# A transformer layer with mixture of experts: the expert tiles moved behind most of the attention, and the norms and ScalarE's work put in another order

## The reference

```python
x = x + layernorm(attention1(layernorm(x), keys, values))     # x: (8, 512, 128); 16 heads of 8, relu projections
x = x + layernorm(encoder(layernorm(x)))

def encoder(x):                       # L = 8 is the sequence, N = 512 tokens are the batch
    y1 = ln(x + mha(x), ln1_g, ln1_b)       # 4 heads of 32, softmax over the 8 rows of the batch axis
    y2 = ln(y1 + moe(y1), ln2_g, ln2_b)
def moe(x):                           # x as 4096 tokens of 128 features, 8 experts
    gates = softmax(x @ wg); idx = argmax(gates); mask = one_hot(idx)
    loc = position of the token among those of its expert; keep = loc < 512
    y = (x @ w1[e] + b1[e]) @ w2[e] + b2[e]     # no activation between: one matrix per expert
    out = gate_val * y if keep else 0
```

## Time and profile before

| | |
|---|---|
| median of 3 runs | 705.54 us (703.77 to 711.51) |
| profiled execution | 711.12 us, span 709.3 us |
| busy over the span | TensorE 562.8 us, VectorE 525.9, ScalarE 396.8, GpSimd 217.1 |
| granted clock of TensorE, mean | 0.88 (1.00 is 2.4 GHz, 0.50 is 1.2 GHz) |

### The profile page before, as it was taken

How to read it: one execution, slowest core, us unless ns; L and a number is a source line. 1 busy time by engine, 2 the same in 40 slices (tenths; PEclk the granted TensorE clock), 3 DMA queues, 4 the chain that set the end, 5 groups by cost and what they waited for, 6 DMA issues and landing times.

```text
span 709.3 us, 9793 instructions
## 1 busy us (share of the span) xinstructions
PE 562.8 (79%) x3475; PEld 206.4 (29%) x3475; DVE 525.9 (74%) x882; ACT 396.8 (56%) x775; POOL 217.1 (31%) x312
## 2 busy tenths in 40 slices
PE   2874999999999999999999777746787588996600
PEld 2650222222222222222222246542444134331100
DVE  4869799999999999999996147495144522869966
ACT  1560699988988889888887523522221110023352
POOL 6001010293324503542228229232220400005341
PEclk9995699999999999999999989966798775978655
DMA  9732011112210112102200020000000000000022
GB/s 251 225 122 101 18 33 34 37 32 63 62 38 28 49 50 62 33 23 70 66 19 10 8 70 1 2 0 0 1 1 0 1 0 1 0 0 0 2 59 59
DMA packets 31393, 28.94 MB, mean 41 GB/s; under 512 B 6240, under 2 KB 23784, under 8 KB 31344
## 3 DMA queue, kind: packets, MB, share of 16 engines
q1 hardware_dynamic: 29312, 27.33, 13.1%
q10 hardware_dynamic: 2032, 0.98, 0.5%
HBM read 19.23 MB, written 8.65 MB: 39 GB/s over the span
## 4 chain that ended last, share of the span: by engine, by line
PE 52%; DVE 25%; ACT 9%; POOL 6%; issue 4%; DMA 2%; ACTq 0%; SPq 0%; DVEq 0%
PE ps L1459 12%; PE ps L1454 9%; PE ps L590 9%; DVE row_max L1631 9%; PE ps L1427 5%; DVE space L922 3%; PE ps L588 3%; PE ps L545 2%; ACT space L835 2%; ACT attended L1579 2%; PE ps L614 2%; ACT space L1563 1%; DVE space L268 1%; DMA w_in<-in_L_ffn_out_proj_w 1%; POOL space L391 1%
## 5 line engine op out<-in xcount | busy, mean ns | idle before, releaser
L1631 DVE TENSOR_REDUCE row_max<-ps 128x2 f32<-128x1024 f32 x256 | 299.4, 1218 | 16.4 <-PE ps L1427 13.6
L1563 ACT ACTIVATE space<-ps 128x512 f32<-128x512 f32 x512 | 271.8, 605 | 47.8 <-PE ps L1454 47.3
L1454 PE MATMUL ps<-space 51*128 51x512 bf16 x512 | 159.0, 387 | 6.6 <-ACT space L1563 3.3
L1459 PE MATMUL ps<-space 128*32 128x512 f32 x1024 | 138.1, 612 | 3.0 <-ACT space L1563 0.7
L1427 PE MATMUL ps<-space 48*128 48x512 bf16 x512 | 128.1, 400 | 14.2 <-DVE row_max L1631 12.5
L590 PE MATMUL ps<-W,space 128*128 128x512 f32 x128 | 89.5, 788 | 0.0
L1454 PEld LDWEIGHTS ps<-space 51*128 51x128 bf16 x512 | 41.1, 94 | 164.6 <-ACT space L1563 144.8
L922 DVE TENSOR_REDUCE space<-ps 128x128 f32<-128x1024 f32 x32 | 39.0, 1220 | 62.4 <-PE ps L590 62.4
L1303 POOL CAST max_parts<-row_max 128x16 bf16<-128x16 f32 x32 | 6.3, 198 | 239.9 <-DVE row_max L1631 239.8
L437 POOL TENSOR_TENSOR space<-PC,same_row 128x512 f32<-128x512 f32 x32 | 32.9, 1059 | 80.1 <-DVE PC L881 80.1
L588 PE MATMUL ps<-c_stack,space 32*128 32x512 bf16 x64 | 28.0, 437 | 24.2 <-DVE space L922 22.7
(11 more groups left out here) (223 smaller groups left out, 708.2 us busy)
## 6 DMA issues: line engine op xcount, KB each, us to landing
q_parts_dram<-space SPq DMA_DIRECT2D x2, 1536.0 KB, 5.4
space<-q_parts_dram SPq DMA_DIRECT2D x64, 48.0 KB
attended_dram<-attended SPq DMA_DIRECT2D x128, 18.0 KB
X<-in_L_attn_queries SPq DMA_DIRECT2D x8, 256.0 KB, 7.6
space<-in_L_ffn_w SPq DMA_DIRECT2D x2, 1024.0 KB, 5.9
space<-q_parts_dram SPq DMA_DIRECT2D x64, 32.0 KB
space<-attended_dram SPq DMA_DIRECT2D x16, 128.0 KB, 2.4
space<-inverses_dram SPq DMA_DIRECT2D x16, 128.0 KB
```

The lines of the kernel that those rows point to most:

```text
L1454: pe.matmul(ps[:, col_bank(v), :], k_rows[rows_a, kappa // 4 % 2, tc * P:(tc + 1) * P], q_stack[rows_a, kappa % 4, b * S:(b + 1) * S], sta ...
L1459: mm = pe.matmul(ps[32 * m:32 * m + 32, PV, :], v_heads[:, tc, PAIR * (kappa // 4) + m % PAIR, :], probs[:, tc % 2, m, :], start=(tc == 0) ...
L1563: act.activation(probs[:, tc % 2, m, :], ps[:, col_bank(v), :], ACT.Exp, scale=1.0 / math.sqrt(DH)).then_inc(s_pr, 1)
L1631: dve.tensor_reduce(row_max[:, par].rearrange("p (a c) -> p a c", a=PAIR)[:, :, item], ring(n), AX.X, MAX).then_inc(s_free, 1)
```

## The change

Tile 0 comes first in half 6. Tiles 0, 1 and 2 stand in half 6 and 3 and 4 in half 7; tiles 0 to 7 take turns in banks 0/1 and 2/3, which the scores no longer need once the last of them are reduced, and all later ones in three pairs of banks. The second part of `spread_turned` uses banks 6 and 7 in every half. The norms of the groups are split into a beginning (`variance1`) and an end (`apply1`), with other work between; the two norms of the last group are begun before the first residual and finished behind it. The second group's tokens are turned ahead of the second scores. The gate weights are begun after selection 21 (23 before). GpSimd's additions on 128 x 1024 are done as two halves. In the tail, variances and scales are in a new order and the last group's fifth norm has buffers of its own. ScalarE's order follows.

In the diff, lines that are only removed in the orders of TensorE, ScalarE and VectorE are left out; they stand in the kernel above.

```diff
...
 BIG = 1e30
-RING = [0, 2, 4]
-EARLY = 2 * B
+EARLY = B
 MASK_ROW = PARTS
...
+def st65(g):
+    return st6 if g == G - 1 else st6p
+def small5(g):
+    return small if g == G - 1 else smallp
...
-LAST1, LAST2, NORM4 = G + 1, G + 2, 2 * G + 2
-LN1 = [G] + [G + 2 + g for g in range(1, G)]
-TAIL = [(4, 0), (4, 1), (5, 0), (4, 2), (5, 1), (5, 2), (4, 3), (5, 3)]
+LAST1, LAST2, NORM4 = G, G + 2, 2 * G + 2
+LN1 = [G + 1] + [G + 2 + g for g in range(1, G)]
+TAIL = [(4, 0), (4, 1), (5, 0), (4, 2), (5, 1), (4, 3), (5, 2), (5, 3)]
...
+    def affine(g, gain, shift, done):
+        for row, op in ((gain, MUL), (shift, ADD)):
+            for lo in (0, QB):
+                half = A[:, g, lo:lo + QB]
+                ins = pool.tensor_tensor(half, half, bcast(rows[:, row, :], QB), op)
+                if op == MUL or lo == 0:
+                    ch.done(ins)
+                else:
+                    ins.then_inc(done, 1)
+            ch.wait()
...
         pool.wait_ge(s_n3, g + 1)
-        ch.done(pool.tensor_tensor(A[:, g], A[:, g], bcast(rows[:, 0, :], B), MUL))
-        ch.wait()
-        pool.tensor_tensor(A[:, g], A[:, g], bcast(rows[:, 1, :], B), ADD).then_inc(s_y1, 1)
+        affine(g, 0, 1, s_y1)
...
         pool.wait_ge(s_wa, g)
-        pool.tensor_tensor(same(A[:, g]), same(A[:, g]), same(YT[:, g]), ADD).then_inc(s_sum, 1)
+        for lo in (0, QB):
+            half = A[:, g, lo:lo + QB]
+            ins = pool.tensor_tensor(half, half, YT[:, g, lo:lo + QB], ADD)
+            ins.then_inc(s_sum, 1)
...
         pool.wait_ge(s_n4, g + 1)
-        ch.done(pool.tensor_tensor(A[:, g], A[:, g], bcast(rows[:, 2, :], B), MUL))
-        ch.wait()
-        pool.tensor_tensor(A[:, g], A[:, g], bcast(rows[:, 3, :], B), ADD).then_inc(s_aff, 1)
+        affine(g, 2, 3, s_aff)
...
-    return 6 if k < EARLY else RING[(k - EARLY) % len(RING)]
+    return 2 * (k % 2) if k < EARLY else 2 * ((k - EARLY) % 3)
...
-    bank, lo = ((6, 0), (5, B * E), (5, B * E), (7, 0))[g]
+    bank, lo = (5, B * E) if g < 2 else (7, 0)
     return ps[:, bank, lo:lo + P // 2].bitcast(BF16)
-LOGITS_BANK = [5, 5, 5, 6]
+LOGITS_BANK = [5, 5, 6, 6]
...
         pe.wait_ge(s_y1, g + 1)
         turn(A[:, g], 6, s_y1t)
+    def tile(k):
+        if k < 2:
+            pe.wait_ge(s_msk, 2 * G)
+        elif k < EARLY:
+            pe.wait_ge(s_sel, k - 1)
+        elif k == EARLY + 2:
+            pe.wait_ge(s_ot, 2 * G)
+            pe.wait_ge(s_lgc, 2)
+        else:
+            pe.wait_ge(s_sel, k - 1 if k < EARLY + 2 else k - 2)
+        if k % B == 0:
+            pe.wait_ge(s_nm, k // B + 1)
+        experts(k)
     first_group(pe, 7)
     pe.wait_ge(s_rm, 1)
     pe.wait_ge(s_qkv, 3)
     scores2(0)
     pe.wait_ge(s_rows, 16 * 6)
     pe.wait_ge(s_pr, COLUMN_ITEMS)
     turn_tokens(1)
+    scores2(1)
+    pe.wait_ge(s_pve, NQ)
     project(1)
+    pe.wait_ge(s_cb, QB)
+    for q in range(2 * G):
+        g, half = q // QPG, q % QPG
         if q >= 1:
             pe.wait_ge(s_ot, q)
+        if q in (0, 2, 4):
+            pe.wait_ge(s_qkv, 3 * (g + 1) + 2)
+        if q in (5, 7):
+            pe.wait_ge(s_lgc, q // 2 - 1)
+        if q == 6:
+            pe.wait_ge(s_nm, 1)
         spread_turned(q, 0, 4)
+        if half == 0:
+            if g < G - 1:
+                pe.wait_ge(s_qkv, 3 * (g + 1) + 3)
+            if g:
+                pe.wait_ge(s_res, g)
         spread_turned(q, 1, 6)
+        if q + 2 < 2 * G:
+            scores2(q + 2)
+        if q == 6:
+            tile(0)
+            tile(1)
+        if q == 7:
+            tile(3)
         attend(q)
         if q == 1:
             project_out(0)
             turn_tokens(2)
             project(2)
         if q == 3:
             turn_y1(0)
+            pe.wait_ge(s_y1c, 2)
             project_out(1)
             turn_tokens(3)
             project(3)
+        if q == 4:
+            route(0)
+        if q == 5:
+            turn_mask(0)
+            turn_y1(1)
+            pe.wait_ge(s_y1c, 4)
+            project_out(2)
+        if q == 6:
+            route(1)
+            tile(2)
+        if q == 7:
+            turn_mask(1)
+            tile(4)
+            project_out(3)
+    for k in range(5, EARLY):
+        tile(k)
+    pe.wait_ge(s_res, G)
+    turn_y1(2)
+    tile(8)
+    tile(9)
+    route(2)
+    tile(10)
+    tile(11)
+    turn_mask(2)
+    for k in range(12, 16):
+        tile(k)
+    for half in range(2):
+        if half == 0:
+            pe.wait_ge(s_lgc, 3)
+        else:
+            pe.wait_ge(s_nm, 3)
+        pe.wait_ge(s_y1l, half + 1)
+        for b in range(QB):
+            mm = pe.transpose(ps[:, 6 + half, b * P:(b + 1) * P], A[:, G - 1, QB * half + b, :], ident[:])
+        mm.then_inc(s_y1t, 1)
+        tile(16 + half)
+    route(G - 1)
+    tile(18)
+    tile(19)
     turn_mask(G - 1)
     pe.wait_ge(s_lgc, G)
     masks = maskp[:].rearrange("p g k c -> p (g k) c")[:, :, MASK_ROW:MASK_ROW + 2 * E]
     pe.matmul(ps[:, 6, 0:T * E], upper[:], masks, start=True, stop=True)
     pe.matmul(ps[:, 6, T * E:2 * T * E], all_ones[:], masks, start=True, stop=True).then_inc(s_cnt, 1)
+    for k in range(20, T):
+        tile(k)
 def back_end_act(act):
     def copy_tokens(g, bank=4):
...
     copy_tokens(1)
     softmax_exp(0)
+    project(1, lambda: softmax_exp(1))
+    copy_turned(0, 0, 4)
+    copy_turned(0, 1, 6)
+    copy_attended(0)
+    softmax_exp(2)
+    copy_turned(1, 0, 4)
+    copy_turned(1, 1, 6)
+    copy_attended(1)
+    softmax_exp(3)
     copy_tokens(2)
+    root(act, LAST1, smallo)
+    project(2, lambda: root(act, LN1[0]))
     copy_turned(2, 0, 4)
     copy_turned(2, 1, 6)
     copy_attended(2)
+    root(act, LAST2, smallo)
     copy_turned(3, 0, 4)
     copy_turned(3, 1, 6)
     softmax_exp(4)
     copy_attended(3)
     copy_y1(0, 6)
+    softmax_exp(5)
+    copy_tokens(3)
+    project(3, lambda: root(act, LN1[1]))
+    copy_turned(4, 0, 4)
+    copy_turned(4, 1, 6)
+    copy_attended(4)
+    softmax_exp(6)
     copy_logits(0)
     copy_turned(5, 0, 4)
+    copy_turned(5, 1, 6)
+    copy_attended(5)
+    softmax_exp(7)
     copy_y1(1, 6)
+    copy_turned(6, 0, 4)
+    copy_turned(6, 1, 6)
+    root(act, LN1[2])
+    copy_attended(6)
     copy_logits(1)
     copy_turned(7, 0, 4)
+    copy_turned(7, 1, 6)
+    copy_attended(7)
+    root(act, LN1[3])
     copy_y1(2, 6)
     copy_logits(2)
     for half in range(2):
         act.wait_ge(s_y1t, G + half)
         act.copy(same(YT[:, G - 1, QB * half:QB * half + QB]), ps[:, 6 + half, :]).then_inc(s_y1c, 1)
...
     apply4 = lambda g, which=range(B): apply(g, s_i4, small4(g), s_n4, which)
-    apply5 = lambda g, which=range(B): apply(g, s_i5, smallp, s_n5, which)
+    apply5 = lambda g, which=range(B): apply(g, s_i5, small5(g), s_n5, which)
     root4 = lambda g: root(act, tail(4, g), small4(g))
-    root5 = lambda g: root(act, tail(5, g), smallp)
+    root5 = lambda g: root(act, tail(5, g), small5(g))
...
     apply5(1)
+    root4(3)
+    apply4(3, range(0, B, 2))
     root5(2)
     apply5(2)
-    root4(3)
-    apply4(3, range(0, B, 2))
     root5(3)
...
-    def ln1(g):
+    def variance1(g):
         dve.wait_ge(s_res, g + 1)
-        norm(dve, ch, LN1[g], tiles(A, g), tiles(A, g)).then_inc(s_n3, 1)
+        norm_variance(dve, ch, tiles(A, g), st6, small)
+    def apply1(g):
+        norm_invert(dve, ch, LN1[g], small)
+        norm_apply(dve, tiles(A, g), tiles(A, g), small).then_inc(s_n3, 1)
...
         dve.tensor_reduce(YT[:, k // B, k % B, :], ps[:, bank:bank + 2, :].rearrange("p a (d e) -> p (a d) e", e=E),
                           AX.X, MAX).then_inc(s_sel, 1)
+    last = G - 1
     compact(0)
     normalise(0)
+    dve_invert(dve, last)
     for q in range(1, 2 * QPG):
         compact(q)
         normalise(q)
+    dve.wait_ge(s_r1, G)
+    norm_variance(dve, ch, tiles(A, last), st6o, smallo)
     residual(0)
+    variance1(0)
+    norm_invert(dve, ch, LAST1, smallo)
+    ch.done(norm_apply(dve, tiles(A, last), tiles(A, last), smallo))
+    ch.wait()
+    ch.done(dve.tensor_tensor(X[:, last], X[:, last], A[:, last], ADD))
+    apply1(0)
+    ch.wait()
+    norm_variance(dve, ch, tiles(X, last), st6o, smallo)
     compact(4)
+    norm_invert(dve, ch, LAST2, smallo)
+    norm_apply(dve, tiles(X, last), tiles(A, last), smallo).then_inc(s_n2l, 1)
     normalise(4)
     compact(5)
     normalise(5)
+    residual(1)
+    variance1(1)
+    apply1(1)
     compact(6)
     normalise(6)
+    choose(0)
     compact(7)
     normalise(7)
+    copy_others(0)
+    residual(2)
+    variance1(2)
+    select(0)
+    apply1(2)
+    select(1)
+    select(2)
+    choose(1)
+    select(3)
+    select(4)
+    copy_others(1)
     g = G - 1
     residual(g)
     dve.wait_ge(s_res, G)
     norm_variance(dve, ch, tiles(A, g), st6, small)
+    select(5)
     norm_invert(dve, ch, LN1[g], small)
     for lo in (0, QB):
         bs = range(lo, lo + QB)
...
```

(117 more changed lines are left out.)

70 lines of the change are left out of this document (2 added, 68 removed).

## The result

The changed kernel takes 663.61 us (median of 4 runs, 657.12 to 663.98) against 707.16 for the kernel before on the same occasions. The ratio is 0.936, interval 0.928 to 0.944: faster. The forecast was 660. The profiled execution took 663.98 us, 47.1 less than the one before, where I had forecast 46.

The account below looks back on a forecast made before the run. TensorE and VectorE waited on each other over one bank pair between residuals 1 and 3; stages gave -62, slow clock +16, so -46: 665 us profiled, 660 as median, range 639 to 684.

Parts of the forecast that it names:

- 26.4 + 26.1 + 58.1: Residual 1 to 2, 2 to 3 and 3 to gate: forecast us at full clock, against 68.8, 58.7 and 26.4 before.
- the clock's +16: TensorE ahead of the gate: 28% of 22 tiles slow costs 14 us, one slow projection 2 more.
- The idle 2.5 us for the last group's choice: Residual 3 to gate: TensorE stands 2.5 us until the last group's choice is made.
- Sum -8.7, to 65.9: Gate to end: two more selections +2.4, halved additions -7.5, earlier variances and own buffers -3.6.
- Halves of 1.17 us leave about half of it: Tail: halving GpSimd's additions cuts about 15 us of VectorE's stall excess by 7.5, bounds 0 and -9.
- waits of 3.3 and 2.4 us shrink: Tail: variances begun ahead of tiles and separate scale buffers for the last group shorten waits, -3.6 us.
- rival (c): Tail gives nothing back: VectorE gets in only behind both halves, selections eat the variances' gain; 669 us, chance 0.07.
- (a): Clock worse than now: attention halves without tiles idle TensorE, 60% of 22 tiles slow; 680 us, chance 0.13.
- (d): Slower than before: 22 tiles ahead of the gate in a row, all at 1.2 GHz; 716 us, chance 0.03.
- I take 0: Start of back end to residual 0: earlier attention half used up by VectorE's statistics; 0 us, bounds -3.4 and +2.
- -10.2 for the norms: Residual 0 to 1: last group's norms fill VectorE's 8.9 us root wait; bounds -6 and -12 us.
- Rival (b): Engine orders don't interlock: ScalarE stands at roots, two waits of 8.9 us give +18; 678 us, chance 0.14.

Follow-up runs that it names:

- b: Changed kernel with the tail's order of variances, scales and roots and the fifth norm's shared buffers as before, halved additions kept: 659.72 us, ratio 0.935.
- d: Changed kernel with the norms at the start of the back end in one piece again, ScalarE's roots moved to match: 664.43 us, ratio 0.939.
- i: Changed kernel with only the start of the back end as before (second scores ahead of the turned tokens, second exponential behind the projections): 662.72 us, ratio 0.937.
- j: Changed kernel with front, norms, GpSimd's additions and tail order undone together, leaving the tile move: 672.25 us, ratio 0.951.
- f: Changed kernel with all 32 expert tiles in one pair of banks, each waiting for the selection of the tile before: 706.13 us, ratio 0.995.
- a: Changed kernel with GpSimd's gain, shift and sum additions whole again instead of halved: 664.99 us, ratio 0.940.
- c: Changed kernel with both the old tail order and GpSimd's whole additions: 665.89 us, ratio 0.942.
- l: Changed kernel with choice and gate sum earlier, plus the fourth norm's gain and shift of groups 0 to 2 on VectorE: 644.88 us, ratio 0.913.
- g: Changed kernel with no expert tile in halves 6 and 7; tiles 0 to 4 follow the last output projection: 670.93 us, ratio 0.949.
- k: Changed kernel with the last group's choice behind selection 17 and the gate sum behind selection 18: 651.60 us, ratio 0.921.

## Why the prediction was right, and where it wasn't

Up to the gate the mechanism was right in the main, but 660 was met partly by luck: two errors of opposite sign nearly cancelled. At the full clock I had 26.4 + 26.1 + 58.1 between residual 1 and the gate; b, d, i and j ran the last of these in 58.4 or 58.5. f shows that a hand-over costs 1.39 us for each tile, where I had 1.34. For sixteen tiles that is 21 to 22 of the 37 us gained between residual 1 and the gate, and expert matmuls of 724 instead of 777 ns give about 5 (both estimates); the rest no run separates. With the clock's +16 the gate was due near 590 and came at 582.1; the end was due 70 us or less behind it and came 76.5 behind. The idle 2.5 us for the last group's choice came as written.

The two terms were the tail and the clock. **The tail**, "Sum -8.7, to 65.9", measured 76.5: +10.6. The step that failed is "Halves of 1.17 us leave about half of it". I counted a stall as a price of each instruction, so that half the piece cost half; a, b and c showed that a dependent chain is held as long as GpSimd has work: 21.0 us of excess with halves against 21.9 with whole additions in the new order, 14.7 against 16.8 in the old. The other half of the step, "waits of 3.3 and 2.4 us shrink", was right in itself (9.8 to 3.9 us of waits), but b showed that the variances moved into GpSimd's additions and paid it back. This is rival (c), with another mechanism than the one I named.

**The clock**, +16, measured about 7 in the tile stage of the profiled execution and 0.3 in others, and about 3.4 more between residuals 1 and 2 (a projection of 5.37 us for 3.70, turns of 3.65 us for 1.95). I took the share of slow expert matmuls from before. In the tiles up to the gate they now average 724 ns, against 777 before, and 661 in experiment i. In f, where nearly every tile waits for a hand-over, they average 758: the handing over may have brought part of the slow share, but no run shows how much. Rivals (a) and (d) are out.

A smaller term was wrong twice: the output projection was put at 3.8 us in both stages between residuals 1 and 3, from rows of before (3.79) that were slow; at the full clock it took 2.05 and 1.95. It hides part of the clock's cost in the first of these stages and makes the second 23.8 us where I had 26.1.

**The norms and the front** were credited the wrong way round: "I take 0" for the front, -10.2 for the norms. By the stages of d, i and j, residual 1 moved by 10.7 us from the start of the back end (70.2 to 59.5); undoing the norms costs 4.3 of it, undoing the front 5.9. The front's transposes ran straight behind the first scores. Rival (b) did not come: while the attention ran, ScalarE stood for 2.3 us ahead of one root (437.54) and 1.3 us ahead of another (452.63), and a table load took 1.28 us, against two waits of 8.9 in the rival.

## What to carry to other kernels

Count a hand-over between two engines per tile and buffer before judging the order of work: here most of the gain was gone with one pair of banks for all tiles (f), and what the order alone gives was not measured. Where one engine's stalls come from a port that another holds, cutting the other's work into pieces changes little (0.9 of 21.9 us, 2.1 of 16.8); move that work to another engine (l), or the dependent chain out of its time (14.7 us in the order of b against 21.0, though waits took its place there). And look for idle time of the engine that bounds the end in the stage ahead of it: 11 to 12 us came from starting its last sum three tiles earlier, with the choice that it needs.

## What the runs showed of the hardware

The small instruction let through differs with the cut. With whole additions the second and third independent small instructions pass unstalled (0.16 us each); with halves the third is stalled (1.24). An 8-column TENSOR_SCALAR with a single input stalls as well (1.24 us at 604.07), as do those with two; a reduction from PSUM doesn't (1.21 us at 607.67). The Trainium skill, SBUF — State Buffer, Who interferes with whom, says just that: instructions with two SBUF inputs and tensor_scalar in its two-port modes contend, tensor_reduce on this chip never does. The trace agrees, though no run shows in which mode the small TENSOR_SCALAR ran. What the page does not lead one to expect is that cutting GpSimd's work leaves most of the sum of the stalls.

The clock fell to half at 562.24 us, with TensorE in unbroken work for over 30 us (since a wait of 0.8 us at 529.9), a routing and half a tile the last of it. The Trainium skill, TensorE: Matmul & The Clock Gate, HAM oscillation — how this bites in real kernels, puts the half rate down to idle gaps; this fall has none ahead of it, so the trace does not agree for it. It agrees for another: behind the 2.5 us wait for the last group's choice, expert matmuls ran at half clock within 3 us in all eight profiled versions that have the wait (the changed kernel, a to d, g, i and j), and not in k and l, which don't have it. Of the 20 routings of groups 2 and 3 in those ten versions, six were followed by slow matmuls within 2 us of their end. Nor is the clock a property of the program alone. The same tile stage granted 0.97 on average in i and 0.87 in the changed kernel's profile, 58.4 and 64.8 us, and medians of kernels that differ by 5 us in one stage came out alike.
